# One projection for the keys of two heads, and a score tile with its second pass in two 64-row matmuls

## The chip, the cores and the metric

The kernel runs on one core of one Trainium2 chip. Its time is the device time of one execution in microseconds; before the change it is 985.65 us, the median of three runs (984.38 to 986.23). The engines of the core are TensorE (PE, with PEld for its weight loads), VectorE (DVE), ScalarE (ACT), GpSimd (POOL) and SyncE (SP), which issues most transfers.

## The reference

The program is one transformer layer: cross attention with 16 heads, then a feed-forward part with ternary weights. Of the attention, for two batches of 512 queries and 1024 context rows:

```python
q_hk = (hidden_q @ Wq.T).reshape(Bv, Sv, H, K)
q_big = jnp.einsum('bshk,hkq->bshq', q_hk, w_kc_q)
q_big = _apply_rope(q_big, sin_q[None, :, None, :], cos_q[None, :, None, :])
kv_r = _apply_rope(kv_c, sin_k[None], cos_k[None])
q_r = jnp.einsum('bshq,hqr->bhsr', q_big, W_qr)
k_r = jnp.einsum('bld,hdr->bhlr', kv_r, W_kr)
scores = jnp.einsum('bhsr,bhlr->bhsl', q_r, k_r)
attn = jax.nn.softmax(scores, axis=-1)
ctx_c = jnp.einsum('bhsl,bld->bhsd', attn, kv_r)
ctx_lat = jnp.einsum('bhsd,hkd->bhsk', ctx_c, w_kc_kv)
ctx = ctx_lat.transpose(0, 2, 1, 3).reshape(Bv, Sv, H * K)
return ctx @ Wo.T
```

Queries and keys of a head have R = 64 numbers each. The scores of one head and batch are a 512 x 1024 matrix with a sum over these 64. What follows the attention (a layer norm, two projections with ternary weights, silu, a third projection) is not touched.

## The kernel before

**Precision.** Every operand of a product is held as two parts, hi (the value in the reduced type fp32r) and lo (what hi leaves), and a product is hi x hi + lo x hi + hi x lo, three matmuls (`three`, L852 to L856). After each product ScalarE copies the result from its bank to the hi part (`high_part`, L637 to L655), and VectorE subtracts to get the lo part (`take_out`, L721 to L745).

**Work of a head.** Products of a head are named by a letter and numbers (batch b, tile or half):
- A(b): x times Wq, 12 matmuls of 512 columns. B(b, c): three chunks of the expanded queries, 3 matmuls each; VectorE multiplies them by the rotary tables, GpSimd adds, splits and stores them (`rotate`). C(b): the queries, 6 matmuls (L884 to L891), summed over the rotated chunks.
- K(b, half): keys of a batch, 512 at a time, 3 matmuls each, four groups per head. The weights are given twice side by side (L892 to L896), so rows 0 to 63 and rows 64 to 127 of the result both hold the head's 64 numbers.
- score u, eight tiles of 128 queries and 1024 keys (`score_tile`, L924 to L941): the stationary operand is qr, 128 rows, query hi above query lo. The moving one is kr_hi and then kr_lo, each 128 rows with the keys twice. So a tile is four matmuls of 128 rows and 512 columns.
- max u on VectorE, exp u on ScalarE, T(u, half) the transposes of the exponentials (4 of 128 columns each), V(b) the values (24 matmuls), M the product of two weights, O(b, j) the output tiles (3 matmuls each), which VectorE adds to `acc`.

**What sets the order.** The order is written out by hand in `SCHEDULE` (from L66), one list that TensorE, ScalarE and VectorE all follow, each taking its own items from it. "next" marks a product of the next head that is made ahead and "last" one of the head before that is made late. GpSimd has its own order (`gpsimd_heads`, period, L611 to L632), and so has SyncE. Heads 1 to 14 run in a hardware loop of seven turns with two heads in each; head 0 and head 15 stand apart, the last one in a second block.

**Banks.** The scores have two double banks. All other products share four banks: the long kinds A, C, V one (number 3), the short kinds B, K, T, M, O the other three in turn (`banks_of`, L136). A product can start when the one that used its bank before has been read by VectorE: a wait on `group_read`, which counts the groups in order.

## Time and profile before

| | |
|---|---|
| runs, median (lowest to highest) | 985.65 us (984.38 to 986.23) |
| profiled execution, its own time | 986.32 us |
| its span, first to last instruction | 984.5 us |
| TensorE busy | 879.4 us, 89% |
| VectorE busy | 838.0 us, 85% |
| ScalarE busy | 489.3 us, 50% |
| GpSimd busy | 514.8 us, 52% |
| mean granted TensorE clock | 0.955 |
| heads 1 to 14, from about 110 to 760 us | TensorE busy throughout |

A timeline row gives the start and the length of an instruction in us, the engine, the line of the kernel, the operation, what it writes and reads, and in brackets how long its engine sat idle before it and what ended that. Matmuls overlap: a matmul's row is longer than the distance to the next one's start, and the distance is what it costs. What ran around the change can be read by its tiles: banks<-kt,wk are keys, scores<-kr,qr scores, banks<-ident,probs transposes, banks<-m,cv outputs, banks<-pt,v values, banks<-x,wq A, banks<-rot,wr C.

### The profile page before, as it was taken

To read this page: it belongs to the slowest core of one execution; us is meant where nothing else is said; L and a number is where in the kernel's file an instruction comes from. 1 tells how busy PE (TensorE), PEld (TensorE's weight loads), DVE (VectorE), ACT (ScalarE), POOL (GpSimd) and SP (SyncE) were. 2 spreads that over 40 slices of the span, in tenths; PEclk is the share of its full clock that TensorE was granted. 3 is DMA by queue.
4 is the path that set the end of the run, shared out by engine and by line. 5 is a ranking of instruction groups with operands and counts; after the bars stand their busy time and mean duration, and the time that the engine had idled before them with its cause. 6 is when DMAs were issued, how large, how long until landed. Compare 5 with 4: busy or idle time off the path is not lost. (4 is left out here: it accounts for less than half of the span.)

```text
span 984.5 us, 15195 instructions
## 1 busy us (share of the span) xinstructions
PE 879.4 (89%) x4381; PEld 685.6 (70%) x4390; DVE 838.0 (85%) x1232; ACT 489.3 (50%) x801; POOL 514.8 (52%) x543
## 2 busy tenths in 40 slices
PE   3649999999999999999999999999999776149996
PEld 3437888888888888888888888888888654014443
DVE  6659898989898889999898989898989566979995
ACT  2225455445454545555554545455545587774432
POOL 5277565656565556464646556565656103605541
PEclk9779999999999999999999999999999899559998
DMA  7000000000000101000000000000000650400000
GB/s 272 0 25 25 14 25 14 26 14 24 13 24 13 26 14 30 19 21 16 24 13 24 13 24 24 13 24 13 24 13 24 239 201 4 178 0 12 21 22 32
DMA packets 18262, 38.35 MB, mean 39 GB/s; under 512 B 1600, under 2 KB 8000, under 8 KB 16960
## 3 DMA queue, kind: packets, MB, share of 16 engines
q1 hardware_dynamic: 17152, 35.99, 11.0%
q10 hardware_dynamic: 1088, 2.10, 0.6%
q8 instruction: 11, 0.18, 0.1%
q14 instruction: 11, 0.09, 0.0%
HBM read 35.98 MB, written 2.10 MB: 39 GB/s over the span
## 5 line engine op out<-in xcount | busy, mean ns | idle before, releaser
L664 ACT ACTIVATE probs<-scores,neg_max 128x1024 f32<-128x1024 f32 x128 | 144.1, 1126 | 141.3 <-DVE neg_max L778 140.2
L655 ACT CAST pt_hi<-banks 128x512 fp32r<-128x512 f32 x256 | 144.7, 595 | 126.4 <-PE banks L920 126.4
L745 DVE TENSOR_TENSOR pt_lo<-banks,pt_hi 128x512 fp32r<-128x512 f32 x256 | 169.4, 683 | 20.0 <-ACT pt_hi L655 19.8
L575 POOL TENSOR_TENSOR rot_cos<-rot_cos,rot_sin 128x512 f32<-128x512 f32 x93 | 120.2, 1293 | 117.0 <-DVE rot_sin L754 106.1
L778 DVE TENSOR_REDUCE neg_max<-scores 128x1 f32<-128x1024 f32 x128 | 155.7, 1218 | 1.0
L920 PE MATMUL banks<-ident,probs 128*128 128x128 f32 x1024 | 143.9, 274 | 6.6 <-DVE rot_sin L754 2.3
L920 PEld LDWEIGHTS banks<-ident,probs 128*128 128x128 f32 x1024 | 123.4, 141 | 33.6 <-DVE acc L773 2.8
L583 POOL TENSOR_TENSOR rot_lo<-rot_cos,rot_hi 128x512 fp32r<-128x512 f32 x93 | 119.8, 1288 | 7.8
L937 PE MATMUL scores<-kr_hi,qr 128*128 128x512 f32 x256 | 109.1, 426 | 9.2 <-PEq L983 5.1
L937 PE MATMUL scores<-kr_lo,qr 128*128 128x512 f32 x256 | 102.1, 399 | 0.0
L855 PE MATMUL banks<-pt_hi,v_hi 128*128 128x512 f32 x256 | 100.6, 393 | 1.6 <-DVE pt_lo L745 1.6
L855 PE MATMUL banks<-pt_hi,v_lo 128*128 128x512 f32 x256 | 100.7, 393 | 0.0
L855 PE MATMUL banks<-pt_lo,v_hi 128*128 128x512 f32 x256 | 100.5, 392 | 0.0
L773 DVE SCALAR_TENSOR_TENSOR acc<-banks,inv,acc 128x512 f32<-128x512 f32 x128 | 92.9, 747 | 7.8 <-PE banks L855 7.3
L1432 POOL TENSOR_TENSOR hidden<-sigma,val 128x512 f32<-128x512 f32 x32 | 46.4, 1451 | 60.0 <-DVE val L1346 53.7
L1306 PE MATMUL ps_gv<-ternary,xt 128*128 128x512 bf16 x251 | 59.2, 391 | 14.2 <-PEq L1081 13.2
L752 DVE TENSOR_TENSOR rot_cos<-banks,cos 128x512 f32<-128x512 f32 x96 | 65.8, 685 | 3.5 <-POOL rot_lo L583 2.9
L581 POOL TENSOR_SCALAR rot_hi<-rot_cos 128x512 fp32r<-128x512 f32 x93 | 57.6, 620 | 15.8 <-POOL rot_cos L575 7.5
L855 PE MATMUL banks<-x_hi,wq_hi 128*128 128x512 f32 x128 | 54.8, 428 | 8.0 <-DVE x_lo L404 6.8
L230 POOL TENSOR_SCALAR wv_hi<-load 128x128 fp32r<-128x128 f32 x15 | 4.5, 298 | 109.5 <-PE banks L855 109.5
L937 PEld LDWEIGHTS scores<-kr_hi,qr 128*128 128x128 f32 x256 | 49.0, 191 | 18.0 <-issue 5.3
L855 PEld LDWEIGHTS banks<-pt_hi,v_hi 128*128 128x128 f32 x256 | 48.5, 189 | 12.6 <-DVE pt_lo L745 2.2
(176 smaller groups left out, 1913.6 us busy)
## 6 DMA issues: line engine op xcount, KB each, us to landing
load<-in_pack SPq DMA_DIRECT2D x15, 320.0 KB, 2.9
load<-in_pack SPq DMA_DIRECT2D x16, 256.0 KB, 2.7
raw_early<-in_gate_w SPq DMA_DIRECT2D x4, 1024.0 KB, 8.1
raw_early<-in_val_w SPq DMA_DIRECT2D x4, 1024.0 KB, 15.9
load<-in_pack SPq DMA_DIRECT2D x16, 192.0 KB, 2.4
acc<-in_x ACTq DMA_DIRECT2D x4, 512.0 KB, 7.6
load<-in_pack SPq DMA_DIRECT2D x16, 128.0 KB, 2.1
raw_early<-in_out_w SPq DMA_DIRECT2D x2, 1024.0 KB, 22.2
```

Of the source, the lines that this page charges most:

```text
L575: nc.gpsimd.tensor_tensor(total, total, rot_sin[:, c, :], ALU.add).then_inc(rot_sum, 1)
L583: nc.gpsimd.tensor_tensor(lo, total, hi.bitcast(F32), ALU.subtract).then_inc(rot_ready, 1)
L655: nc.scalar.copy(out, src).then_inc(group_hi, 1)
L664: nc.scalar.activation(probs[:, u % 2, :], scores[:, u % 2, :], ACT.Exp, bias=neg_max[:, u:u + 1], accum_out=sums[:, u:u + 1]).then_inc(ex ...
L745: return nc.vector.tensor_tensor(pair[1], src, pair[0].bitcast(F32), ALU.subtract)
L752: nc.vector.tensor_tensor(rot_cos[:, c, :], src, t["cos"][:, c, :], ALU.mult)
L773: return nc.vector.scalar_tensor_tensor(out=t["acc"][:, u, :], in0=src, scalar=inv[:, u:u + 1], in1=t["acc"][:, u, :], op0=ALU.mult, op1=A ...
L778: nc.vector.tensor_reduce(neg_max[:, u:u + 1], scores[:, u % 2, :], AX, ALU.max, negate=True).then_inc(max_ready, 1)
L855: mm = nc.tensor.matmul(out, ws[a], xs[c], start=first and n == 0, stop=last and n == 2)
L920: mm = nc.tensor.transpose(out[:, c * P:(c + 1) * P], probs[:, u % 2, at:at + P], t["ident"][:])
L937: mm = nc.tensor.matmul(scores[:, u % 2, half * 512:(half + 1) * 512], qr[:, b, j * P:(j + 1) * P], kr[low][:, b, half * 512:(half + 1) * ...
L1306: mm = nc.tensor.matmul(ps_gv[:, n % 4, :], x, w[:, c, part_of(n // 2)], start=c == 0, stop=c == KD - 1)
```

## The change

1. *Keys of two heads in one product.* The weights `wk` now hold three pieces of 64 columns: even head, odd head, even head. K(b, 0) uses the first two and K(b, 1) the last two, so that a group of 3 matmuls gives 512 keys of both heads, one in rows 0 to 63 and the other in rows 64 to 127. `schedule_of` drops the groups that are no longer needed: a head of even number makes K(1, 0) and K(1, 1), an odd one makes K(0, 0) and K(0, 1) for the next pair. Head 15 makes none.
2. *Where the parts lie.* `kr_even` and `kr_odd` take the place of `kr_hi` and `kr_lo`. Each holds one head's keys, hi in one half of the rows and lo in the other (the other way round for the second 512 keys). ScalarE fills the hi parts with two copies of 64 rows, and VectorE the lo parts with two subtractions of 64 rows, from one half of the rows to the other.
3. *Score tile.* `qr_hi` holds query hi in both halves of the rows, `qr_lo` query lo in both. The first pass multiplies qr_hi with 128 rows of keys, hi and lo at once. The second multiplies query lo with key hi alone, 64 rows, rows 0 to 63 for one half of the keys and rows 64 to 127 for the other. The product lo x lo is no longer formed.
4. *Queries.* ScalarE makes two copies of query hi in place of one. VectorE's two steps are as before and fill rows 64 to 127 of qr_lo. A new item "double" is a ScalarE copy of these to rows 0 to 63.
5. *Loading.* Once per pair of heads three transfers bring the key weights to `wk_raw`, and GpSimd splits them in two instructions of 192 columns, instead of two of 128 columns per head.
6. *Space and order.* q and cv share one buffer; O(1, 3) stands ahead of A(1)'s second part. GpSimd's split of the next weights waits for T(1, 1) and not for K(1, 1).

```diff
@@ SCHEDULE
-    ("exp", 0), ("exp", 1), part(1, 2, V1), ("T", 0, 0), ("K", 1, 0),
+    ("exp", 0), ("double", 1, "last"), ("exp", 1), part(1, 2, V1), ("T", 0, 0), ("K", 1, 0),
...
-    ("score", 3), ("max", 3), ("K", 1, 1), ("T", 1, 1), ("O", 1, 2, "last"), part(1, 2, A1), ("T", 2, 0),
-    ("T", 2, 1), ("exp", 3),
-    ("score", 4), ("B", 1, 0, "next"), ("O", 1, 3, "last"), ("T", 3, 0), part(0, 3, C0), part(1, 3, C0),
+    ("score", 3), ("max", 3), ("K", 1, 1), ("T", 1, 1), ("O", 1, 2, "last"), ("O", 1, 3, "last"), part(1, 2, A1),
+    ("T", 2, 0), ("T", 2, 1), ("exp", 3),
+    ("score", 4), ("B", 1, 0, "next"), ("T", 3, 0), part(0, 3, C0), part(1, 3, C0),
...
-    ("score", 6), ("exp", 5), part(0, 8, V0), part(1, 8, V0), part(2, 8, V0), part(3, 8, V0), ("max", 6),
+    ("score", 6), ("exp", 5), ("double", 0, "next"), part(0, 8, V0), part(1, 8, V0), part(2, 8, V0), part(3, 8, V0), ("max", 6),
@@ schedule_of
+        if group[0] == "K" and (group[1] == 0) != odd:
+            return False
...
+        schedule.insert(schedule.index(("exp", 2)), ("double", 1))
@@ weight_splits
-        split(h, 3, [w[:] for w in t["wk"]], twice(src, CQ * R, 1)).then_inc(wk_ready, 1)
+
+    def key_pair(h):
+        pool.wait_ge(t["pair_loaded"], h.pairs(48))
+        pool.nop(nofuse=True)
+        nc.gpsimd.tensor_scalar(t["wk"][0][:], t["wk_raw"][:], 1.0, 0.0, ALU.mult, ALU.add).then_inc(t["pair_hi"], 1)
+        pool.wait_ge(t["pair_hi"], h.pairs(1))
+        nc.gpsimd.tensor_tensor(t["wk"][1][:], t["wk_raw"][:], t["wk"][0][:].bitcast(F32), ALU.subtract).then_inc(wk_ready, 1)
@@ attention_heads
-        qr = sb("qr", [P, B, S], F32R)
-        kr = [placed(f"kr_{x}", [P, B, L], F32R) for x in ("hi", "lo")]
+        qr = [placed(f"qr_{x}", [P, B, S], F32R) for x in ("hi", "lo")]
+        rest = nc.alloc_sbuf_tensor_at("rest", [P, B, S], F32, offset=at["qr_lo"])
+        kr = [placed(f"kr_{x}", [P, B, L], F32R) for x in ("even", "odd")]
...
-        q = [sbe(f"q_{x}", [P, S], F32R) for x in ("hi", "lo")]
+        q = cv
...
+        def keys_at(group):
+
+            _, b, half = group
+            one, other = (x[:, b, half * 512:(half + 1) * 512] for x in (kr[half], kr[1 - half]))
+            return (slice(0, R), one), (slice(R, 2 * R), other)
@@ high_part (ScalarE)
                 elif kind == "C":
-                    out, src = qr[0:R, group[1], :], banks[0:R, p.bank[marked], :]
+                    src = banks[0:R, p.bank[marked], :]
+                    nc.scalar.copy(qr[0][0:R, group[1], :], src)
+                    out = qr[0][R:2 * R, group[1], :]
                 elif kind == "K":
-                    out = kr[0][:, group[1], group[2] * 512:(group[2] + 1) * 512]
+                    (up, into_up), (down, into_down) = keys_at(group)
+                    nc.scalar.copy(into_up[up], banks[up, p.bank[marked], :])
+                    out, src = into_down[down], banks[down, p.bank[marked], :]
...
+            def double(p, marked):
...
+                act.wait_ge(group_read, p.read(done))
+                nc.scalar.copy(qr[1][0:R, b, :], qr[1][R:2 * R, b, :]).then_inc(doubled, 1)
@@ take_out (VectorE)
+                    if kind == "K":
+                        (up, into_up), (down, into_down) = keys_at(group)
+                        nc.vector.tensor_tensor(into_up[down], banks[up, bank, :], into_up[up].bitcast(F32), ALU.subtract)
+                        return nc.vector.tensor_tensor(into_down[up], banks[down, bank, :], into_down[down].bitcast(F32),
+                                                       ALU.subtract)
@@ products and score_tile (TensorE)
-                    pe.wait_ge(wk_ready, h.after(1, 1))
+                    pe.wait_ge(wk_ready, h.pairs(1))
                     at = group[1] * L + group[2] * 512
-                    mm = three(out, [w[:, 0].rearrange("p o r -> p (o r)") for w in wk],
+                    mm = three(out, [w[:, group[2] * R:(group[2] + 2) * R] for w in wk],
                                [t[x][:, at:at + 512] for x in ("kt_hi", "kt_lo")])
...
-                for half in range(2):
-                    for low in range(2):
+                odd = p.head.number % 2
+                if not odd:
+                    pe.wait_ge(group_read, p.read(p.place(("K", 1, 1)) if b else p.earlier(("K", 0, 1, "next"))))
+                pe.wait_ge(doubled, p.head.after(B, b + 1))
+                for low in range(2):
+                    for half in range(2):
+
+                        rows = slice(R * (half ^ odd), R * (half ^ odd) + R) if low else slice(0, P)
                         mm = nc.tensor.matmul(scores[:, u % 2, half * 512:(half + 1) * 512],
-                                              qr[:, b, j * P:(j + 1) * P],
-                                              kr[low][:, b, half * 512:(half + 1) * 512],
+                                              qr[low][rows, b, j * P:(j + 1) * P],
+                                              kr[odd][rows, b, half * 512:(half + 1) * 512],
                                               start=low == 0, stop=low == 1)
```

The order in which instructions stand, at three places of an even head of the loop. A row of it gives the line, the operation, what is written and read (names of the program: kt the rotated context turned round, m and cv the operands of O, ident and probs those of T), the size, and in brackets the semaphores waited for. The first place is TensorE at score 3, before:

```order
L920 MATMUL banks<-ident,probs 128x128 [waits exp_ready]
L920 MATMUL banks<-ident,probs 128x128 x3
L937 MATMUL scores<-kr_hi,qr 128x512 [waits group_read,exp_ready]
L937 MATMUL scores<-kr_lo,qr 128x512
L937 MATMUL scores<-kr_hi,qr 128x512
L937 MATMUL scores<-kr_lo,qr 128x512
```

and after the change:

```order
L974 MATMUL banks<-ident,probs 128x128 [waits exp_ready]
L974 MATMUL banks<-ident,probs 128x128 x3
L992 MATMUL scores<-kr_even,qr_hi 128x512 [waits doubled,group_read,exp_ready]
L992 MATMUL scores<-kr_even,qr_hi 128x512
L992 MATMUL scores<-kr_even,qr_lo 128x512 x2
```

Four matmuls of 128 rows have become two of these and, in the last row, two of 64 rows on qr_lo (the size given is that of the result), and the tile also waits for the new copy.

The second place follows directly behind it on TensorE: K(1, 1), T(1, 1), O(1, 2) and what comes then. Before:

```order
L855 MATMUL banks<-kt_hi,wk_hi 128x512 [waits wk_ready,group_read]
...
L920 MATMUL banks<-ident,probs 128x128 [waits exp_ready,group_read]
L920 MATMUL banks<-ident,probs 128x128 x3
...
L855 MATMUL banks<-m_hi,cv_hi 128x512 [waits group_read]
L855 MATMUL banks<-m_lo,cv_hi 128x512
L855 MATMUL banks<-m_hi,cv_lo 128x512
L855 MATMUL banks<-x_hi,wq_hi 128x512 [waits wq_ready]
```

and after the change:

```order
L909 MATMUL banks<-kt_hi,wk_hi 128x512 [waits wk_ready,group_read]
...
L974 MATMUL banks<-ident,probs 128x128 [waits exp_ready,group_read]
L974 MATMUL banks<-ident,probs 128x128 x3
...
L909 MATMUL banks<-m_hi,cv_hi 128x512 [waits group_read]
L909 MATMUL banks<-m_lo,cv_hi 128x512
L909 MATMUL banks<-m_hi,cv_lo 128x512
...
L909 MATMUL banks<-m_hi,cv_hi 128x512 [waits group_read]
L909 MATMUL banks<-m_lo,cv_hi 128x512
L909 MATMUL banks<-m_hi,cv_lo 128x512
L909 MATMUL banks<-x_hi,wq_hi 128x512 [waits wq_ready]
```

O(1, 3) has moved up. It uses the same one of the three short banks as K(1, 1), and waits for `group_read`; before the change A(1)'s second part stood there, which waits only for its weights.

The third place is VectorE behind V(1), where it takes out the values, T(0, 0) and K(1, 0). Before:

```order
L745 TENSOR_TENSOR cv_lo<-banks,cv_hi 128x512 [waits group_hi]
L726 REGISTER_ALU
L745 TENSOR_TENSOR pt_lo<-banks,pt_hi 128x4x128 [waits group_hi]
L726 REGISTER_ALU
L745 TENSOR_TENSOR kr_lo<-banks,kr_hi 128x512 [waits group_hi]
L769 RECIPROCAL inv<-sums 128x4 [waits exp_ready]
```

and after the change:

```order
L799 TENSOR_TENSOR cv_lo<-banks,cv_hi 128x512 [waits group_hi]
L777 REGISTER_ALU
L799 TENSOR_TENSOR pt_lo<-banks,pt_hi 128x4x128 [waits group_hi]
L777 REGISTER_ALU
L788 TENSOR_TENSOR kr_even<-banks,kr_even 64x512 [waits group_hi]
L789 TENSOR_TENSOR kr_odd<-banks,kr_odd 64x512
L823 RECIPROCAL inv<-sums 128x4 [waits exp_ready]
```

One subtraction of 128 rows (kr_lo) has become two of 64 rows, and only the second is counted as having read the bank.

## Rows read from the trace of the kernel before

**Rows 1.** The page, busy time of each engine (us, share of the span, instructions)
```profile
PE 879.4 (89%) x4381; PEld 685.6 (70%) x4390; DVE 838.0 (85%) x1232; ACT 489.3 (50%) x801; POOL 514.8 (52%) x543
```

**Rows 2.** Busy time by stretch: us and instructions of PE, PEld, DVE, ACT, POOL; PEclk, DMA
```profile
310.00:410.00 100.00, 100.00 (x506) 82.53 (x505) 89.56 (x131) 50.13 (x92) 59.14 (x66) 1.00 0.07 18
```

**Rows 3.** Timeline, GpSimd, one instruction in two heads (start us, us, engine line op, idle)
```profile
341.10 0.62 POOL L230 TENSOR_SCALAR wq_hi<-load 128x512 fp32r<-128x512 f32 x1
...
388.11 0.62 POOL L230 TENSOR_SCALAR wq_hi<-load 128x512 fp32r<-128x512 f32 x1
```

**Rows 4.** Timeline, TensorE, a score tile behind transposes
```profile
302.50 0.48 PE L937 MATMUL scores<-kr_hi,qr 128*128 128x512 f32 x1
302.82 0.40 PE L937 MATMUL scores<-kr_lo,qr 128*128 128x512 f32 x1
303.06 0.40 PE L937 MATMUL scores<-kr_hi,qr 128*128 128x512 f32 x1
```

**Rows 5.** Timeline, VectorE, two 64-row halves of one product
```profile
309.68 0.69 DVE L755 TENSOR_TENSOR rot_sin<-banks,sin 64x512 f32<-64x512 f32 x1
310.39 0.68 DVE L756 TENSOR_TENSOR rot_sin<-banks,sin 64x512 f32<-64x512 f32 x1
```

**Rows 6.** Timeline, the second key group of batch 0, all engines
```profile
341.45 0.40 PE L855 MATMUL banks<-kt_hi,wk_hi 128*128 128x512 f32 x1
...
342.35 0.58 ACT L655 CAST kr_hi<-banks 128x512 fp32r<-128x512 f32 x1 [0.58 <-PE banks L855]
...
342.96 0.69 DVE L745 TENSOR_TENSOR kr_lo<-banks,kr_hi 128x512 fp32r<-128x512 f32 x1 [0.48 <-ACT kr_hi L655]
...
343.71 0.19 PEld L855 LDWEIGHTS banks<-m_hi,cv_hi 128*128 128x128 f32 x1 [0.24 <-DVE kr_lo L745]
```

**Rows 7.** Timeline, the queries of batch 1 and the next first projection
```profile
343.31 0.59 ACT L655 CAST qr<-banks 64x512 fp32r<-64x512 f32 x1
...
344.28 0.68 DVE L731 TENSOR_TENSOR rest<-banks,qr 64x512 f32<-64x512 f32 x1
...
345.82 0.19 PEld L855 LDWEIGHTS banks<-x_hi,wq_hi 128*128 128x128 f32 x1 [0.21 <-issue]
```

**Rows 8.** Timeline, behind the values of batch 1: keys, then a transpose
```profile
311.41 0.48 PE L855 MATMUL banks<-kt_hi,wk_hi 128*128 128x512 f32 x1
...
311.87 0.69 DVE L745 TENSOR_TENSOR cv_lo<-banks,cv_hi 128x512 fp32r<-128x512 f32 x1 [0.80 <-ACT cv_hi L655]
...
313.07 0.68 DVE L745 TENSOR_TENSOR kr_lo<-banks,kr_hi 128x512 fp32r<-128x512 f32 x1
...
314.49 0.60 PE L920 MATMUL banks<-ident,probs 128*128 128x128 f32 x4
```

**Rows 9.** Timeline, the second key group of batch 1
```profile
317.43 1.12 ACT L664 ACTIVATE probs<-scores,neg_max 128x1024 f32<-128x1024 f32 x1
...
317.67 0.39 PE L855 MATMUL banks<-kt_hi,wk_hi 128*128 128x512 f32 x1
...
318.56 0.58 ACT L655 CAST kr_hi<-banks 128x512 fp32r<-128x512 f32 x1
...
319.31 0.68 DVE L745 TENSOR_TENSOR kr_lo<-banks,kr_hi 128x512 fp32r<-128x512 f32 x1
...
319.50 0.40 PE L855 MATMUL banks<-x_hi,wq_hi 128*128 128x512 f32 x1
```

**Rows 10.** Timeline, GpSimd from M to the last rotated part, and its reader
```profile
328.16 0.30 POOL L230 TENSOR_SCALAR wv_hi<-load 128x128 fp32r<-128x128 f32 x1 [7.55 <-PE banks L855]
...
339.85 1.28 POOL L583 TENSOR_TENSOR rot_lo<-rot_cos,rot_hi 128x512 fp32r<-128x512 f32 x1
...
342.50 0.48 PE L890 MATMUL banks<-rot_hi,wr 128*128 128x512 f32 x1
```

**Rows 11.** Timeline, TensorE, the last head
```profile
793.19 1.25 PE L920 MATMUL banks<-ident,probs 128*128 128x128 f32 x8 [1.62 <-DVE kr_lo L745]
```

**Rows 12.** Timeline, TensorE, before the first head
```profile
38.05 0.80 PE L855 MATMUL banks<-x_hi,wq_hi 128*128 128x512 f32 x1 [5.37 <-DVE x_lo L404]
```

More of the change, by code:

```diff
@@ L64 @@
 A0, A1, V1, V0, C0, C1 = ("A", 0, "next"), ("A", 1, "next"), ("V", 1, "last"), ("V", 0), ("C", 0, "next"), ("C", 1, "next")
-UNGROUPED = ("score", "max", "exp", "sum")
+UNGROUPED = ("score", "max", "exp", "sum", "double")
 SCHEDULE = (
@@ L105, in plus, with pairs @@
         return Head(self.number + n, self.i)
+    def pairs(self, per_pair):
+        fixed = (self.number // 2 + 1) * per_pair
+        return fixed if self.i is None else self.i * per_pair + fixed
 def done_by(item):
@@ L167, in __init__ @@
         else:
-            self.schedule = schedule_of(self.first, self.last)
-            self.order, self.bank = order_of(self.schedule), BANK
+            odd = head.number % 2
+            self.schedule = schedule_of(odd, self.first, self.last)
+            self.order, self.bank = order_of(self.schedule), BANK[odd]
             if self.first:
@@ L173, in __init__ @@
             else:
-                self.before = [(g, BANK[g]) for g in ALL]
+                self.before = [(g, BANK[1 - odd][g]) for g in ALL[1 - odd]]
                 self.start = head.after(GROUPS, GROUPS_BEFORE)
@@ L533, in period @@
             def period(p):
+                if p.head.number % 2:
+                    load_key_pair(p.head.plus(1))
                 load_lot(p.head.plus(1), WVO)
@@ L565, in split_wr_wk @@
                 splits[WRK](h, load)
+                if h.number % 2 == 0:
+                    splits[PAIR](h)
             def split_wv_wo(h):
@@ L600, in prepare @@
                 first_split(WRK, start.first_loaded[WRK])
+                splits[PAIR](p.head)
                 rotate_here(0, 2, None)
@@ L682, in prepare @@
                 high_part(p, ("C", 0))
+                double(p, ("double", 0))
                 start.values_high(act, 1)
```

85 lines of the change are left out of this document (47 added, 38 removed).

## The prediction

> **What bounds the kernel now.** I read the page first, then the busy time by stretch, then the timeline of one head on each engine, and last the waits. The page shows TensorE busy 89% of the span and VectorE 85% [rows 1]. In the 100 us from 310 on, TensorE is busy all the time at full clock and VectorE 89.6% [rows 2]; the other stretches between 110 and 760 us are alike. Sixteen heads follow each other. The same GpSimd instruction of two neighbouring heads stands at 341.10 and 388.11, so a head takes 47.0 us [rows 3]. The reader is to see two things. TensorE sets this time, since it never waits for long. But VectorE has only some 4.8 us per head to spare (47.0 x 10.4%), and every product passes through one of four banks that ScalarE and VectorE must first empty. So what the change saves on TensorE counts only as far as the banks are free earlier.
>
> A 512-column matmul starts 0.24 us after the one ahead, though it is recorded as 0.40 long; behind transposes the first takes 0.32 [rows 4]. Over longer stretches it is 0.23: a key group, a group of transposes and an output product fill 317.67 to 319.50 [rows 9] as 3 x 0.23 + 0.44 + 3 x 0.23 = 1.82. I write 0.23 for a pass of 512 columns, 0.69 for a product of three.
>
> **The change, part by part.** My letters are the kernel's: K keys, C queries, A first projection, V attention values, O output, T transpose, M weight product; the numbers are batch, tile or half. A head of even number now makes only K of batch 1, an odd one only K of batch 0.
>
> *TensorE.* Keys: 12 matmuls per head become 6, which takes away 6 x 0.23 = 1.38 us. Scores: per tile, four full passes become two full ones and two of 64 rows. If those two run side by side they cost one pass, and eight tiles save 8 x 0.23 = 1.84 us. A head's TensorE work is then 47.0 - 3.2 = 43.8 us.
>
> *The hand-over of keys.* This is the change's price. ScalarE copies a key group in two halves and only the second signals; VectorE subtracts in two halves that move between partition halves. ScalarE's copies start 0.48 apart back to back (two of them from 342.35 to 343.31) [rows 6, 7], so its signal comes 0.48 later. Two VectorE instructions of 64 rows that shift partitions start 0.71 apart [rows 5], where two of 128 rows took from 311.87 to 313.07, 0.60 each [rows 8]; so a group takes 1.42. Per head that is two groups instead of four, 2.8 against 2.4 us, nearly nothing in busy time. But one group is now released 0.48 + 0.71 = 1.2 us later, and the third short product behind it needs its bank. A queries group adds one ScalarE copy (0.48) ahead of VectorE as well. The two "double" copies per head (2 x 0.5 us) stand where ScalarE idles for VectorE's maximum and I cost them at nothing; without that cover they would put off one exponential by 0.5.
>
> I walk through a pair of heads, in the trace's times.
>
> *Odd head.* (1) The V1 copy goes into the buffer that O(1,0) reads. VectorE starts it at 311.87 [rows 8], its reader is released 0.75 after such a start (342.96 to 343.71 in rows 6): 312.62. With K(1,0) gone, TensorE has only a transpose (0.44 with the slower first matmul) and a score tile (0.69) after V1 ends at 311.05 (one transpose group ahead of 311.41, rows 8), and arrives at 312.18. It waits 0.5. (2) K(0,1) to O(0,3): the weight load had waited 0.24 for this very group, so there is no slack today [rows 6]; 1.2 later means a wait of 1.2, with 0.07 for the exposed weight load 1.3. (3) K(0,0) to T(5,0): 0.2. (4) C1 to the next A: no slack today either (the load sat 0.21) [rows 7]; wait (2) moves TensorE back, 0.1 is left. Together 2.1, the head 43.8 + 2.1 = 45.9.
>
> *Even head.* (5) K(1,0) to T(0,1): VectorE starts at 313.07 today [rows 8], then at about 313.5, and releases at 313.5 + 0.71 + 0.75 = 314.96; TensorE, one score pass earlier, is there at 314.26. Wait 0.8 with the load. (6) K(1,1) to O(1,3), which has moved ahead of A's second part. Today A stands there at 319.50 and waits for no keys. ScalarE can't take the keys before its exponential, 317.43 to 318.56, and VectorE starts at 319.31 [rows 9]. With the second copy and the lateness from (5) it starts near 320.05 and releases at 321.5; TensorE arrives near 319.65 (319.50, three score passes earlier, the wait (5) later, hence 319.50 - 0.69 + 0.85). Wait 1.9 to 2.0. This is the largest term. (7) GpSimd works without a break from M (wv_hi at 328.16) to the last rotated part (339.85 + 1.28 = 341.13), which C1's last part reads at 342.50: slack 1.3 [rows 10]. In an even head TensorE drops three score passes (0.69) and two key groups (1.38) in between: 2.07 - 1.3 = 0.8. (8) C1 to the next A: 0.48 later on ScalarE, a score pass less on TensorE, partly absorbed by (7): 0.3. Together 3.8, the head 47.6.
>
> A pair then takes 93.5 instead of 94.0. So 6.4 us of TensorE work go and 5.9 come back as waits. Where a score pass lies inside one of these windows, making it faster or slower changes nothing; that leaves about 2 tiles of an even and 6 of an odd head that count. The seven pairs of the loop bring 7 x (-0.5) = -3.5 us.
>
> *The cost of turning to 64-row work and back* stands nowhere in this trace. The nearest rows: the first matmul behind transposes starts its follower 0.09 later (0.32 for 0.23) [rows 4], which is an exposed weight load. From below I take nothing (the two 64-row loads hide under the second full pass), from above the whole tail of a matmul, 0.40 - 0.24 = 0.16, with that load, 0.25 a turn and two turns a tile. I take 0.05 a tile, nearest to the row of 0.09, since only some turns should show: 7 x 8 x 0.05 = +2.8.
>
> The Trainium skill, "TensorE: Matmul & The Clock Gate", section "The mechanism", has matmuls on different row groups start about 4 ns apart. No run so far shows it; by it a pair would cost one pass. "TensorEngine Tiling (Array Packing)", section "Key Properties", says that changing the tiling mode drains the array; by it the sum would end on the slower side (rival D, whose price is from the rows above).
>
> *Outside the loop.* Head 0 is even but has no V1 or O waits: between 0 and -3.2, I take -1.5. The last head made K(1,0) and K(1,1) and now makes none; there TensorE sat 1.62 us for K's second part [rows 11]: -2.0 (0 to -3). Its score passes count little, as it waits for others. At the start VectorE subtracts K(0,0) in two parts ahead of x_lo, for which TensorE waits 5.37 us until 38.05 [rows 12]: +0.9, the longer subtraction (0.82), up to +2. The later stages are untouched.
>
> **Sum**, against the profiled execution (986.32 us, span 984.5): -3.5 + 2.8 - 1.5 - 2.0 + 0.9 = -3.3, hence 983.0. The median of the runs is 0.67 lower: 982.3.
>
> **Rivals.**
> A is my forecast. Its own range: with no turning cost 979.5, with 0.11 a tile 985.7, and 4 us either way for waits mis-sized by 0.3 a head: 976 to 990.
> B, the waits are about half as long, because an engine catches up in places that I take as full (VectorE's 10.4% idle speaks for it, the two places with no slack today against it). Then a head drops 3.2 - 1.4 = 1.8: 985.65 - 2.6 - 14 x 1.8 = 958. With no waits at all it would be 938.
> C, the change doesn't do what it says: the 64-row matmuls run one after the other. Each tile costs 0.23 more, four passes as before. By the count above, (2 + 6) x 0.23 = 1.8 a pair, 7 x 1.8 = 13, without the turning term: 982.3 - 2.8 + 13 = 992.5 (990 to 996). Nothing in the trace shows two matmuls side by side, which speaks for it.
> D, slower: every turn between 128-row and 64-row work waits for the array's tail, at the score tiles. Tail 0.16, or 0.25 with the load, twice a tile, gives a tile of 0.69 + 0.32 = 1.01 to 1.19 us against 0.92 before. It decides from 0.10 a turn on, where the tile ceases to be faster than the old one. Over C: 112 tiles x (0.09 to 0.27) = 10 to 30, so 1002 to 1023. Against it: behind transposes no such tail is seen, only 0.09.
> E, the two-part key hand-over starts a chain of waits longer than worked out (each later VectorE step delays the next exponential): 0.8 a head more, 994 to 1000.
>
> **Chances.** A 0.38, B 0.17, C 0.15, D 0.22, E 0.08. This kernel's runs tell a change of about 0.2% (2 us) from none: below 983.7 is faster, above 987.6 slower. A splits into 0.23 faster, 0.09 same and 0.06 slower; B is faster; E, C and D are slower but for 0.08 of the two last, with the waits of A smaller at the same time (0.03 faster, 0.05 same). Faster 0.43, same 0.14, slower 0.43. The range of 8 in 10 leaves out the lower half of B and the upper half of D: 957 to 1008. Cases of both signs hold most of the chance; A's own range is 976 to 990.
>
> **What would show it.** In the changed profile: the third score matmul and the fourth starting together (A) or 0.23 apart (C), and the next full matmul 0.23 behind (A) or 0.4 (D). Key groups: one ScalarE copy and one VectorE start more per group. TensorE's wait for VectorE's keys ahead of an O product, near 1.9 us in even and 1.2 in odd heads; ahead of C1's last part, for GpSimd. Even heads of 47.6 and odd ones of 45.9 us. I am wrong if TensorE stays busy without such waits and the head falls to 44 (B), or if the tile takes over 0.92 us (D).

## The result, and the profile after

Changed kernel: 1023.61 us, median of 4 runs (1021.31 to 1025.91), beside 985.07 us for the kernel before. The ratio is 1.039, 95% interval 1.036 to 1.042: slower. The forecast was 982.3.

The page, and busy time by stretch (columns as in [rows 2]):

```profile
PE 889.9 (87%) x4285; PEld 634.8 (62%) x4294; DVE 846.0 (83%) x1232; ACT 532.6 (52%) x865; POOL 511.1 (50%) x527
```

```profile
310.00:410.00 100.00, 96.84 (x474) 72.30 (x472) 86.90 (x124) 54.13 (x98) 53.58 (x59) 1.00 0.07 19
```

There are 96 fewer matmuls than in [rows 1], yet TensorE is busy 10.5 us longer, and it now has gaps where [rows 2] had none (96.84 of 100 us). PEclk reads 1.00 in both, so the clock is not the cause in the loop. The GpSimd instruction of [rows 3] stands 98.28 us apart over two heads, for 94.0 before:

```profile
308.60 0.63 POOL L242 TENSOR_SCALAR wq_hi<-load 128x512 fp32r<-128x512 f32 x1
...
406.88 0.63 POOL L242 TENSOR_SCALAR wq_hi<-load 128x512 fp32r<-128x512 f32 x1
```

Seven pairs of heads make 30 of the 39.6 us between the two profiled spans (1024.1 and 984.5). The forecast hung on two things. The first is the tile, here TensorE's matmuls and weight loads:

```profile
316.31 0.71 PE L992 MATMUL scores<-kr_odd,qr_hi 128*128 128x512 f32 x2
316.95 0.50 PE L992 MATMUL scores<-kr_odd,qr_lo 64*128 64x512 f32 x2
317.39 0.51 PE L909 MATMUL banks<-cv_hi,wc_hi 128*128 128x512 f32 x1
317.73 0.40 PE L909 MATMUL banks<-cv_lo,wc_hi 128*128 128x512 f32 x1
...
341.27 0.61 PE L992 MATMUL scores<-kr_odd,qr_hi 128*128 128x512 f32 x2
341.82 0.49 PE L992 MATMUL scores<-kr_odd,qr_lo 64*128 64x512 f32 x2
...
316.95 0.19 PEld L992 LDWEIGHTS scores<-kr_odd,qr_lo 64*128 64x128 f32 x2 [0.37 <-issue]
...
317.38 0.19 PEld L909 LDWEIGHTS banks<-cv_hi,wc_hi 128*128 128x128 f32 x1 [0.24 <-issue]
```

The two 64-row matmuls are one row of 0.50 us, where two full ones make a row of 0.71: they do run side by side. But the next full matmul starts 0.44 after them, not 0.23, and its own follower 0.34 after it, not 0.23. Ahead of them, the two full passes of the tile at 341.27 take 0.55 us for 2 x 0.23, which is 0.09 for the turn in. (The tile at 316.31 stands behind transposes, which cost another 0.09 before the change too [rows 4], hence its 0.64.) Each weight load of the other kind begins only with its matmul; between full matmuls it runs 0.2 to 0.25 ahead (317.73 has its load at 317.49). So a tile is 0.46 for two full passes, 0.09 for the turn in, 0.44 for the two 64-row matmuls and what follows them, and 0.11 for the turn out: 1.10 us against 0.92 before.

The second is the keys' hand-over, K(1,1) in an even head, and K(0,1) in an odd one (in time order on each engine):

```profile
382.04 0.58 ACT L688 CAST kr_odd<-banks 64x512 fp32r<-64x512 f32 x1
382.64 0.58 ACT L696 CAST kr_even<-banks 64x512 fp32r<-64x512 f32 x1
...
383.25 0.68 DVE L788 TENSOR_TENSOR kr_odd<-banks,kr_odd 64x512 fp32r<-64x512 f32 x1 [0.38 <-ACT kr_even L696]
383.95 0.69 DVE L789 TENSOR_TENSOR kr_even<-banks,kr_even 64x512 fp32r<-64x512 f32 x1
...
384.69 0.50 PE L909 MATMUL banks<-m_hi,cv_hi 128*128 128x512 f32 x1 [1.55 <-DVE kr_even L789]
...
357.07 0.58 ACT L696 CAST kr_even<-banks 64x512 fp32r<-64x512 f32 x1
...
358.38 0.69 DVE L789 TENSOR_TENSOR kr_even<-banks,kr_even 64x512 fp32r<-64x512 f32 x1
359.13 0.50 PE L909 MATMUL banks<-m_hi,cv_hi 128*128 128x512 f32 x1 [1.09 <-DVE kr_even L789]
```

The weight loads of these two matmuls waited 1.99 and 1.53 us; in [rows 6] the same load waited 0.24. The waits by what ended them, from 160 to 710 us (total us, times, longest):

```profile
PEld scores L992 <- issue: 32.7, 90, 0.4
PEld banks L909 <- DVE kr_even L789: 21.1, 12, 2.0
PEld banks L909 <- issue: 16.1, 62, 0.4
PE banks L909 <- DVE kr_even L789: 15.8, 12, 1.6
```

"issue" is time in which the engine waited for nothing that the profile shows. Here it stands ahead of the 64-row loads of 90 score tiles and of the first full load behind 62 of them: these are the turns. The keys' wait comes 12 times, once a head.

### The profile page after: what moved, and what is told of

The parts are those of the page before. It is cut to its first block and busy times, and to the rows that moved or that the text cites. A ratio compares the mean times of both kernels' runs of the same rounds, so it can differ in the third digit from the quotient of the medians.

```text
span 1024.1 us, 15165 instructions
## 1 busy us (share of the span) xinstructions
PE 889.9 (87%) x4285; PEld 634.8 (62%) x4294; DVE 846.0 (83%) x1232; ACT 532.6 (52%) x865; POOL 511.1 (50%) x527
## 5 line engine op out<-in xcount | busy, mean ns | idle before, releaser
L974 PE MATMUL banks<-ident,probs 128*128 128x128 f32 x1024 | 146.6, 276 | 12.6 <-DVE kr_odd L789 3.4
L974 PEld LDWEIGHTS banks<-ident,probs 128*128 128x128 f32 x1024 | 120.8, 141 | 48.6 <-DVE pt_lo L799 7.4
L799 DVE TENSOR_TENSOR cv_lo<-banks,cv_hi 128x512 fp32r<-128x512 f32 x64 | 44.3, 691 | 75.0 <-ACT cv_hi L696 74.5
L909 PE MATMUL banks<-pt_hi,v_hi 128*128 128x512 f32 x256 | 103.5, 404 | 1.6 <-DVE pt_lo L799 1.6
L696 ACT CAST cv_hi<-banks 128x512 fp32r<-128x512 f32 x64 | 37.5, 586 | 116.3 <-PE banks L909 116.3
L909 PE MATMUL banks<-m_hi,cv_hi 128*128 128x512 f32 x128 | 55.0, 430 | 19.3 <-DVE kr_even L789 18.5
L909 PE MATMUL banks<-x_hi,wq_hi 128*128 128x512 f32 x128 | 55.6, 434 | 10.4 <-DVE x_lo L420 8.5
```

Of the source, the lines that this page charges most:

```text
L696: nc.scalar.copy(out, src).then_inc(group_hi, 1)
L799: return nc.vector.tensor_tensor(pair[1], src, pair[0].bitcast(F32), ALU.subtract)
L909: mm = nc.tensor.matmul(out, ws[a], xs[c], start=first and n == 0, stop=last and n == 2)
L974: mm = nc.tensor.transpose(out[:, c * P:(c + 1) * P], probs[:, u % 2, at:at + P], t["ident"][:])
```

## The experiments

"Pair" is a pair of heads, measured as the distance of the instruction of [rows 3] over two heads inside the loop, "head 0" that from its first to its second place, both from the profiled run, in us. A median and a pair of heads can differ in what they say, since the median also holds head 0, head 15 and the start. All ratios are to the kernel before, on the same chip.

| kernel | pair | head 0 | median us | ratio (95%) |
|---|---|---|---|---|
| before | 94.0 | 44.9 | 984 to 986 | 1 |
| changed | 98.2 | 49.1 | 1023.6 | 1.039 (1.036 to 1.042) |
| a_full_rows | 96.6 | 48.0 | 1010.3 | 1.025 (1.022 to 1.028) |
| b_two_64 | 96.6 | 45.1 | 1004.2 | 1.018 (1.015 to 1.022) |
| b_same_64 | 100.2 | 43.7 | 1033.0 | 1.048 (1.045 to 1.052) |
| b_low_last | 94.0 | 43.4 | 984.7 | 1.000 (0.997 to 1.002) |
| e_one_op | 95.2 | 44.4 | 997.0 | 1.013 (1.010 to 1.016) |
| h_k11_only | 97.0 | 47.2 | 1012.1 | 1.027 (1.024 to 1.030) |
| c_moved | 93.7 | 44.9 | 984.7 | 1.001 (0.999 to 1.002) |
| d_moved_64 | 94.8 | 44.9 | 995.9 | 1.011 (1.008 to 1.013) |
| g_moved_more | 96.6 | 49.4 | 1013.3 | 1.028 (1.025 to 1.031) |
| i_two_moves | 92.9 | 49.6 | 988.8 | 1.002 (1.000 to 1.004) |
| j_max_first | 93.4 | 49.7 | 991.0 | 1.007 (1.005 to 1.010) |
| k_head0 | 93.0 | 44.9 | 986.8 | 1.002 (1.000 to 1.004) |
| m_last_old | 93.0 | 45.0 | 984.3 | 1.000 (0.999 to 1.001) |
| f_busy_last | 98.2 | 49.3 | 1023.4 | 1.039 (1.036 to 1.041) |
| l_head0_busy | 93.0 | 46.2 | 986.5 | 1.002 (1.000 to 1.004) |

Head 0 is one run each, and it differs by 1.5 us between the kernel before and b_low_last, whose medians are the same. So a difference of that size there says little.

### The tile alone

b_low_last puts the low pass last in the kernel before. b_two_64 then gives it 64 rows each, rows 0 to 63 for one half of the keys and 64 to 127 for the other, and b_same_64 the same 64 rows twice; both leave out a part of the low terms. The edit of b_two_64, cut:

```diff
-                for half in range(2):
-                    for low in range(2):
+                for low in range(2):
+                    for half in range(2):
+                        rows = slice(R * half, R * half + R) if low else slice(0, P)
...
-                                              qr[:, b, j * P:(j + 1) * P],
-                                              kr[low][:, b, half * 512:(half + 1) * 512],
+                                              qr[rows, b, j * P:(j + 1) * P],
+                                              kr[low][rows, b, half * 512:(half + 1) * 512],
```

> The kernel before with only the order of a tile's four matmuls changed to that of the changed kernel: both halves with the keys' high part, then both with the low part, all with 128 rows. Theory 1 (it is the turn between 128 and 64 rows): same time as before within 1 us. Rival (it is the order: the accumulation into a bank is interrupted by the other bank): a good part of the 22 us shows here, 995 to 1007 us.

> The kernel before with its score tile alone changed: the pass with the keys' low part comes last and is made of two 64-row matmuls, one on rows 0-63 and one on rows 64-127 (this leaves out part of the product: one half of the low terms for each half of the tile). Everything around the tile is as before, keys and waits too. Theory 1 (turning): 128 tiles by 0.175 us are 22 us more, 1007 us (1003 to 1011). Theory 2 (waits alone): the tile doesn't matter, 983 to 987. Theory 3 (side by side saves as intended, the tile is 0.69 to 0.75 us): 8 x 16 x 0.2 = 25 us less, 960 to 970.

> As the kernel before with the low pass last and as two 64-row matmuls, but both on rows 0-63, so that they can't run beside each other (this leaves out the low terms of rows 64-127). It tells what stands in the 0.44 us of the pair. If they run side by side and 0.21 us of emptying stands beside 0.23 of streaming, two on the same rows take 0.67 us: a tile is 0.23 us longer than with separate rows, 128 x 0.23 = 29 us above the kernel with separate rows, about 1036 us. If they run one after another in both cases, the 0.44 us is 2 x 0.22 and the two kernels take the same time within 2 us.

All three came as the first theory had them. The order of the passes does nothing (984.7). The 64-row pass alone costs 20 us in the kernel before: 2.6 a pair of heads, 0.16 a tile. And with the same rows twice the two matmuls take 0.67 (316.83 to 317.50) where with separate rows they take 0.43 (310.64 to 311.07):

```profile
316.19 0.71 PE L938 MATMUL scores<-kr_hi,qr 128*128 128x512 f32 x2
316.83 0.73 PE L938 MATMUL scores<-kr_lo,qr 64*128 64x512 f32 x2
317.50 0.50 PE L855 MATMUL banks<-q_hi,wc_hi 128*128 128x512 f32 x1
```

```profile
309.99 0.71 PE L938 MATMUL scores<-kr_hi,qr 128*128 128x512 f32 x2
310.64 0.50 PE L938 MATMUL scores<-kr_lo,qr 64*128 64x512 f32 x2
311.07 0.50 PE L855 MATMUL banks<-q_hi,wc_hi 128*128 128x512 f32 x1
```

The first fence is b_same_64, the second b_two_64. One pass more costs 0.24 more, so 0.23 of the 0.44 is one pass and 0.21 is time in which nothing new starts. That this is the array running empty, and not the wait for the weight load that begins so late, no run here separates. Either way a tile with 64-row matmuls pays some 0.4 us for two turns to win 0.23. a_full_rows takes only the 64 rows out of the changed kernel:

```diff
-                        rows = slice(R * (half ^ odd), R * (half ^ odd) + R) if low else slice(0, P)
+                        rows = slice(0, P)
```

> The changed kernel with one expression changed: the second pass of a score tile is made of two 128-row matmuls (the queries' low part stands in both halves, so this adds the product of the two low parts). All else of the change stays. In the trace of the changed kernel the two 64-row matmuls of a tile take 0.44 us together, the turn to them adds 0.09 and the turn back 0.11: a tile is 1.10 us long against 0.92 to 0.97 before. Theory 1 (turning between 128-row and 64-row matmuls empties the array, and this price cancels the shorter keys): each of 128 tiles gets 0.175 us shorter, 22 us in all, 1001 us (997 to 1006, the upper end if the wait for GpSimd, 0.8 us a pair of heads, comes back once the tiles are short). Theory 2 (the tile is not the cause, the time lies in the waits for the keys' longer hand-over alone): the wait takes up what the tile gives, 1020 to 1024 us. Either way 985 would not be reached: some 4.2 us of waits a pair of heads remain.

Neither number was hit: 13 us came back, not 22. A pair got 1.6 shorter where 16 tiles got 2.6 shorter. The missing 1.0 is new waiting: TensorE comes sooner to what isn't ready. T(0,1) waits 0.58 for 0.37, V1's reader 0.24 for 0.13, and T(3,0) some 0.16 more in each head; the rest is in smaller gaps.

### The hand-over of keys

e_one_op copies and subtracts a key group at once in the changed kernel, with 128 rows each, and leaves out the layout of the keys (parts land in the wrong rows). h_k11_only moves K(1,1). Of each edit one part is shown: the ScalarE copies of e_one_op, whose two VectorE subtractions become one in the same way, and the new place of K(1,1).

```diff
-                    (up, into_up), (down, into_down) = keys_at(group)
-                    nc.scalar.copy(into_up[up], banks[up, p.bank[marked], :])
-                    out, src = into_down[down], banks[down, p.bank[marked], :]
+                    out = keys_at(group)[0][1]
```

```diff
-    ("O", 1, 1, "last"), ("T", 0, 1), part(0, 2, A1),
+    ("O", 1, 1, "last"), ("T", 0, 1), ("K", 1, 1), part(0, 2, A1),
```

> The changed kernel with the keys handed over as before the change: one ScalarE copy of 128 rows and one VectorE subtraction of 128 rows a group, in place of two and two of 64 rows (this puts the high and low parts of both heads in the wrong rows: the layout of the keys is left out). The 64-row matmuls and the places of the groups stay. It weighs the hand-over: a group is ready some 0.6 + 0.7 = 1.3 us earlier. Theory (the waits of 1.26 us for K(0,1) in odd heads, 1.7 for K(1,1) in even ones and 0.37 for K(1,0) are the length of the hand-over): the first goes, the second falls to about 0.4, the third goes, so a pair of heads is 3.0 us shorter, 95.2 for 98.2, and the kernel takes about 1000 us (996 to 1004). Rival (the groups would wait for ScalarE's and VectorE's other work anyway, and the place decides): under 1 us a pair, 1016 to 1024.

> The changed kernel with K(1,1) alone moved: from between score 3 and T(1,1) to ahead of the first part of A1, so that A1's six matmuls, T(1,0), score 3 and T(1,1) stand between it and the group that needs its bank. The 64-row instructions and all else stay. Theory (its wait of 1.55 + 0.15 us in even heads is a matter of place): an even head gets 1.4 to 1.9 us shorter, half of that may come back at T(3,0), which then has one group less to hide exp 3 behind; a pair takes 96.4 to 97.4 for 98.2, the kernel 1007 to 1017. Rival (VectorE is full there, the wait turns up whole at T(3,0) or A1): 1020 to 1024.

Both as the theory had it: 3.0 us a pair for the two-part hand-over (997.0), and 1.2 for K(1,1)'s place by itself (1012.1). In h_k11_only an odd head keeps its wait, and K(1,1) itself waits 0.43 in its new place:

```profile
353.43 0.50 PE L909 MATMUL banks<-m_hi,cv_hi 128*128 128x512 f32 x1 [1.08 <-DVE kr_even L789]
372.01 0.66 PE L974 MATMUL banks<-ident,probs 128*128 128x128 f32 x4 [0.19 <-DVE kr_odd L789]
373.10 0.51 PE L909 MATMUL banks<-kt_hi,wk_hi 128*128 128x512 f32 x1 [0.43 <-DVE acc L827]
```

### Full rows and moved groups

c_moved has a_full_rows' tile, d_moved_64 the changed kernel's, both with these moves (cut):

```diff
-("exp", 1), part(1, 2, V1), ("T", 0, 0), ("K", 1, 0),
+("exp", 1), ("K", 1, 0), part(1, 2, V1), ("T", 0, 0),
-("T", 3, 0), part(0, 3, C0), part(1, 3, C0),
+part(0, 3, C0), ("T", 3, 0), part(1, 3, C0),
-part(0..3, 8, V0), ("max", 6), part(4, 8, V0), ("K", 0, 0, "next"), part(5, 8, V0)
+part(0..1, 8, V0), ("max", 6), part(2, 8, V0), ("K", 0, 0, "next"), part(3..4, 8, V0), ("K", 0, 1, "next"), part(5, 8, V0)
```

(and K(1,1) as in h_k11_only; `0..3` stands for a run of parts).

> The kernel with full rows (1010.3 us, a pair of heads 96.6) with the key groups elsewhere in the order: K(1,0) ahead of the second part of V1, K(1,1) ahead of the first part of A1, K(0,0) and K(0,1) behind parts 3 and 5 of V0, and the first part of C0 ahead of T(3,0). Theory (after the shorter keys and full rows are counted, all that is left over the 91.2 us a pair should take, 94.0 less 12 matmuls of 0.23, is waits that follow from where the groups stand): a pair takes 91.5 to 92.5 us and the kernel 965 to 975, faster than before the change. Rival (ScalarE and VectorE have no room for the added 64-row instructions, so that the waits only turn up elsewhere, at the softmax of the tile that follows): a pair stays at 94 or above, 985 to 1005.

> The changed kernel, 64-row matmuls and all, with the same moves of the key groups. Theory (turning and waits simply add): a pair is 16 x 0.163 = 2.6 us longer than with full rows, 94.1 to 95.1, and the kernel takes 985 to 997; even without waits it is then no faster than before the change. Rival (the turning costs only where the array has no other gap, so it overlaps part of what waited): within 8 us of the kernel with full rows and the same moves.

c_moved fell between the two: a pair of 93.7, no faster than before. 2.8 us of keys are gone from TensorE and 2.5 us of waits are left. The largest, in an odd head, shows VectorE's queue: both key groups wait behind the maxima and rotary products, and T(5,0) waits for K(0,1).

```profile
331.15 0.39 PE L909 MATMUL banks<-kt_hi,wk_hi 128*128 128x512 f32 x1
...
333.57 1.23 DVE L832 TENSOR_REDUCE neg_max<-scores 128x1 f32<-128x1024 f32 x1
334.83 0.68 DVE L788 TENSOR_TENSOR kr_even<-banks,kr_even 64x512 fp32r<-64x512 f32 x1
...
337.77 0.65 PE L974 MATMUL banks<-ident,probs 128*128 128x128 f32 x4 [0.78 <-DVE kr_even L789]
```

d_moved_64 took 995.9, inside its range, but not for its reason: turns and waits do not simply add. The turns cost 1.1 a pair of heads there and not 2.6 (11 us in all, with the heads outside the loop).

g_moved_more moves T(5,0) behind score 7, T(0,1) ahead of O(1,0) and C1's last part ahead of T(6,0); i_two_moves only the first two. The first of the moves:

```diff
-    ("T", 4, 1), ("T", 5, 0),
-    ("score", 7), part(0, 3, C1),
+    ("T", 4, 1),
+    ("score", 7), ("T", 5, 0), part(0, 3, C1),
```

> The kernel with full rows and moved key groups (984.7 us, a pair 93.7), with three groups more moved, each where its trace shows TensorE waiting: T(5,0) behind score 7 (it waited 0.78 us for K(0,1)'s subtractions), T(0,1) ahead of O(1,0) (0.24 to 0.5 for V1's low part), the last part of C1 ahead of T(6,0) (A0 waited some 0.2 for C1). Theory (TensorE bounds a pair at 91.2, the rest is single waits): a pair takes 91.7 to 92.8, the kernel 966 to 978, faster than before the change. Rival (VectorE, busy without a gap for the 17 us from C0 to the end of V0 in odd heads, bounds that stretch, and its queue sets the pair): a pair stays above 93.2, 981 to 986.

> The kernel with full rows and moved key groups (984.7 us, a pair 93.7) with T(5,0) behind score 7 and T(0,1) ahead of O(1,0), and C1's last part back where it stood: in the last kernel, with a pair of 96.6, T(6,1) waited 1.60 us a head for T(6,0)'s subtraction, which had come to stand behind C1's copies. Theory (that wait alone made that kernel slow, the two other moves gain their 0.8 and 0.3 to 0.5 us): 2 x 1.6 less and some 0.2 back at A0, a pair takes 92.4 to 93.4, the kernel 974 to 982. Rival (VectorE's queue sets the pair, whatever is moved): a pair 93.6 to 94, 983 to 987.

g_moved_more missed the upper end of its range by 35 us. In the loop, 2.9 a pair of heads, it was a wait that I had not looked for, 1.6 us in every head: T(6,1) waits for T(6,0)'s subtraction, held behind C1's copies. Head 0 took 4.5 us more as well.

```profile
307.99 0.66 PE L974 MATMUL banks<-ident,probs 128*128 128x128 f32 x4 [1.60 <-DVE pt_lo L799]
```

i_two_moves hit its pair (92.9) and missed its time (988.8, forecast 974 to 982). Head 0 took 4.7 us of it (49.6 for 44.9); even without them it would have stood above 982.

### The ends

j_max_first swaps `("max", 2)` and T(0,1) on VectorE; k_head0 puts K(1,1) between O(1,0) and O(1,1); m_last_old is k_head0 with T(0,1) and T(5,0) back in their old places in head 15; f_busy_last and l_head0_busy issue the transposes of tiles 2 and 3 of head 15 three times (in the changed kernel and in k_head0):

```diff
-                    for c in range(4):
+                    for n in range(4 * (3 if p.last and u in (2, 3) else 1)):
+                        c = n % 4
```

> The last kernel with VectorE's maximum of tile 2 ahead of T(0,1)'s subtraction instead of behind it (TensorE's order is unchanged). In the last kernel a pair of heads in the loop took 92.9 us, 1.1 less than before the change, yet head 0 took 49.6 where it takes 44.9: TensorE waited 2.27 and 2.76 us there, and the granted clock of 80 to 88 us was 0.63. Theory (head 0 lost by the order of those two on VectorE, and by the lower clock after its waits): head 0 returns to 44.9 to 46 us, a pair stays at 92.9 to 93.4, the kernel takes 978 to 983. Rival (head 0's waits hang on the start, not on this order): head 0 stays above 48, 985 to 989.

> As the kernel of 988.8 us (full rows, moved groups, a pair 92.9), with K(1,1) between O(1,0) and O(1,1) instead of behind both. In the two kernels before this one head 0 took 49.6 us where it had taken 44.9, because head 0 has no O(1,*) groups: K(1,1) there follows T(0,1) at once in the same bank and waited 2.76 and 5.21 us for it. With K(1,1) in the bank of T(0,0) that wait should go. Theory (head 0's loss, in the changed kernel too, is a bank's hand-over and the lower clock that follows such a wait, not the start): head 0 takes 44.5 to 46.5 us, a pair stays at 92.9 to 93.4, the kernel takes 978 to 984. Rival (head 0's time hangs on when the first lots come in): head 0 stays at 48 to 50, 986 to 990.

> The kernel of 986.8 us (full rows, all moves, a pair 93.05, head 0 44.9) with T(0,1) and T(5,0) back in their old places in the last head alone. In the loop that kernel gained 0.95 us a pair over the kernel before, 6.7 us; in the profiled run the last head's first tile to the next stage's first transposes took 85.6 us for 83.4, with waits of 1.20, 0.63 and 2.67 us where the kernel before has 0.20 to 1.10. Theory (the moves that serve the loop cost the last head, where fewer groups stand between, some 2 to 3 us): with the old places these waits go, that stretch takes 83 to 84.5 us and the kernel 983 to 985. Rival (the last head is set by the softmax and by the clock, not by these places): 986 to 988.

> The changed kernel with TensorE kept busy in the last head: the transposes of tiles 2 and 3 are issued three times over there (the same result each time; 32 transposes more, 3.6 us of TensorE's time, put where it waited 1.5, 1.0 and 1.9 us). Theory (the last head is 3.8 us longer than before the change because TensorE idled before M, and the clock then granted was 0.50 to 0.74 for 13 us): no stretch at a lower clock follows, and from score 4 of the last head on its matmuls are 0.23 us apart; the stretch from the last head's first tile to the first matmul of the next stage takes 62 to 64.5 us for 65.8, and the whole 1020 to 1023. Rival (the low clock has another cause): the stretch at a low clock stays, and the last head gets longer by what of the 3.6 us doesn't fit the waits, 1023 to 1027.

> The same kernel with the transposes of tiles 2 and 3 of the last head issued three times over (same result), 3.6 us of work where TensorE otherwise waits some 5 us. Theory (as in the changed kernel, whose last head became 1.8 us shorter by this, the granted clock stays up when TensorE is kept busy): the stretch of 8 us behind tile 3 shows a clock of 1.00 where it was 0.79 to 0.81, and the kernel takes 1 to 3 us less than the one beside it, 976 to 982. Rival (the added work eats what the clock gives): the same within 1 us, or up to 3 us longer.

*Head 0.* j_max_first: the theory fell, head 0 stayed at 49.7, and the wait got longer (5.21 us, for 2.76 in i_two_moves). k_head0: with another bank for K(1,1) head 0 is at 44.9 and the pair at 93.0, as forecast, though the wait is shorter (1.79) and not gone, and the time (986.8) is not the forecast one. So for head 0 of these moved kernels it was the bank: head 0 has no O(1,*), and K(1,1) came right behind the transposes that hold it. In the changed kernel K(1,1) stands elsewhere, and e_one_op speaks for its head 0. j_max_first, then k_head0:

```profile
83.12 0.79 PE L909 MATMUL banks<-kt_hi,wk_hi 128*128 128x512 f32 x1 [5.21 <-DVE pt_lo L799]
```

```profile
80.51 0.50 PE L909 MATMUL banks<-kt_hi,wk_hi 128*128 128x512 f32 x1 [1.79 <-DVE pt_lo L799]
```

*Head 15.* From its first score tile to the next stage's first transposes: before 83.4 us, changed 87.4 (808.81 to 896.18), f_busy_last 85.6. Busy time and granted clock of three stretches, the changed kernel and then f_busy_last:

```profile
828.00:835.00 7.00, 3.39 (x21) 2.28 (x21) 4.17 (x7) 5.13 (x8) 0.00 (x0) 0.96 1.02 392
835.00:841.00 6.00, 6.00 (x14) 3.35 (x15) 4.35 (x5) 4.92 (x6) 0.00 (x0) 0.50 0.13 45
841.00:848.00 7.00, 7.00 (x26) 5.56 (x25) 0.25 (x1) 1.83 (x5) 0.00 (x0) 0.74 0.00 0
```

```profile
828.00:835.00 7.00, 5.33 (x43) 4.68 (x44) 3.34 (x5) 4.01 (x6) 0.00 (x0) 1.00 1.02 390
835.00:841.00 6.00, 5.30 (x28) 3.47 (x27) 4.19 (x6) 4.70 (x9) 0.00 (x0) 1.00 0.05 18
841.00:848.00 7.00, 6.82 (x37) 5.30 (x35) 2.92 (x5) 5.55 (x11) 0.00 (x0) 1.00 0.00 1
```

Behind the idle stretch the clock was at 1.2 GHz (0.50) and with useless work in it at 2.4 GHz (1.00); 1.8 us of the stretch came back in the profiled run, but the median (1023.4) doesn't tell it from nothing. Behind tile 3 in k_head0, and then in l_head0_busy:

```profile
796.00:804.00 8.00, 7.76 (x27) 6.32 (x28) 4.86 (x6) 6.56 (x9) 0.00 (x0) 0.79 0.02 5
```

```profile
797.00:805.00 8.00, 7.29 (x42) 6.00 (x43) 4.57 (x6) 6.61 (x10) 0.00 (x0) 1.00 0.01 4
```

The clock rose to 1.00, as the theory had it, but no time came back (986.5 for 986.8), which is what the rival said. M (banks<-wo_hi,wv_hi) started 31.1 us behind the head's first tile, for 27.9 in k_head0, so the added transposes cost more than the 1 to 3 us that the clock was to give. m_last_old got its time (984.3) but not its reason: the stretch that should shrink to 83 to 84.5 took 86.3 in the profiled run, for 85.6 in k_head0. The runs of k_head0 spread from 984.2 to 990.4, so what the last head costs it stays open, and so does why 1.0 us less for a pair of heads, 7 us over the loop, showed in no median. No version beat the kernel before.

## Why the prediction was wrong

*The score tile.* This step failed. Right: the two 64-row matmuls run side by side. Wrong: "a score tile (0.69)" with "0.05 a tile" for turning. Measured: 1.10 a tile, 0.41 more. Over the 16 tiles of a pair of heads that is 6.6 us, where the forecast had 0.4 (0.05 for each of the 8 tiles that it thought would count). Less the 1.6 by which the waits came out smaller, this gives 4.6; a pair of heads missed by 4.3 (98.2 for 93.9), 30 us over the loop. The other 11 of the 41 us missed are head 0 and head 15. My lower bound supposed that the 64-row weight loads hide under the full pass; they don't (the load engine stands still for 0.37 us ahead of them and for 0.24 behind, once each in a tile). I took the row of 0.09 for the whole price because the trace had a row for it, and gave the bound of 0.25 a turn only the rival. The turns sum to 0.41 a tile, 0.09 in, 0.21 ahead of the next full matmul, 0.11 behind it, against my upper bound of 0.50. b_two_64 shows that this cost is not hidden: with nothing but the 64-row pass changed, the kernel is 20 us longer.

*The rivals.* D named this cost with 1.01 to 1.19 a tile and 1002 to 1023 us; the tile came out inside, the time just above. "TensorEngine Tiling (Array Packing)", section "Key Properties", in the Trainium skill says that a change of tiling mode drains the array. The 20 us of b_two_64 agree with that, though they don't show what the array does. Rival C is dead by b_same_64: matmuls one after the other take 0.67, these 0.44. "TensorE: Matmul & The Clock Gate", section "The mechanism", in the Trainium skill has matmuls on different row groups start about 4 ns apart. The trace agrees as far as one row of 0.50 for both can tell. B had half the waits (about 3 a pair of heads) and a fast tile; the waits were 4.3 and the tile slow. E had more waiting than forecast; there was less.

*Keys on TensorE*, -1.38 a head: right; 94.0 - 2.8 + 16 x 0.17 + the waits of 4.3 is the 98.2 seen (0.17 is what a tile takes over the old 0.92: 0.16 by b_two_64, 0.18 by the rows).

*Waits*, 5.9 a pair forecast, 4.3 seen by this sum. (2) 1.3: 1.26 seen. (6) 1.9 to 2.0: 1.7. (5) 0.8: 0.37; (1) 0.5: 0.13; (3) 0.2: none; (4) and (8) together 0.4: 0.15. (7), 0.8 for GpSimd: none; the tiles that had to be faster were slower, which may be why. Not foreseen: T(3,0) waits 0.25 in the odd and 0.26 in the even head for exp 3; O(1,3) had moved from ahead of it, which no run tests by itself. The mechanism, a longer hand-over in a place with no slack, is shown by e_one_op, which took 3.0 of the 4.3 away. ScalarE's two copies stand 0.60 apart, not 0.48, and VectorE's two subtractions 0.70, as forecast. That only a part of the tiles' time counts where waits stand was right in kind: 1.6 of 2.6 in a_full_rows, 1.1 of 2.6 in d_moved_64. (The spare time of VectorE, given as 4.8 us a head, is 4.9 by its own terms, 47.0 x 10.4%; no term of the sum uses it.)

*Outside the loop.* Head 0: -1.5 forecast, +4.2 seen; e_one_op takes it to 44.4, so it is mostly the keys' hand-over (a_full_rows, with the old tile, leaves it at 48.0), and between 80 and 96 us TensorE is busy 11.6 of 16 us for 15.0 before. Head 15: -2.0 forecast, +3.9 seen. An estimate puts 1.3 of it on the eight slower tiles (8 x 0.16 from b_two_64), and 1.8 was gone in the one profiled run with the clock up; the rest is open. The start: +0.9 forecast; the first wq_hi behind it stands between 61.2 and 63.1 us in all 17 profiled runs, whichever keys they use (61.2 before the change, 63.1 after it, 63.0 in m_last_old), so it can't be told.

*The range.* The likeliest case let turning vary only from 0 to 0.11 a tile, though its price was the one that stood in no row; the bounds were 0 and 0.50, and the likeliest case should have spanned them.

## What to carry to other kernels

A cost that no row shows deserves the widest bounds, not the value of the nearest row: here 0.05 a tile, which should have been 0.41, came 112 times in the loop. One pair of 64-row matmuls between full ones did not pay here: it won one pass of 0.23 and paid 0.41. By these numbers, and this is an estimate that no run tests, two such pairs in a row (0.46 won) would about break even. And taking work off the busiest engine of a balanced kernel can move the wait to the next queue: 2.8 us less on TensorE for a pair of heads were never worth more than 1.1.

## What the runs showed of the hardware

- Two 512-column matmuls on rows 0 to 63 and 64 to 127 together take 0.43 to 0.44 us between full ones (b_two_64 and the changed kernel), two on the same rows 0.67 (b_same_64).
- Turning from 128-row to 64-row matmuls and back costs 0.41 us in the changed kernel, and no weight load of the other kind runs ahead: it starts with its matmul (316.95, 317.38), where loads between full matmuls start 0.2 to 0.25 us ahead.
- Half the rows did not make an instruction shorter. Two ScalarE copies of 64x512 start 0.60 us apart (382.04 and 382.64) and two VectorE subtractions 0.70 (383.25 and 383.95); two of 128x512 start 0.48 and 0.60 apart before the change [rows 6, 7, 8]. For ScalarE the gap goes with the change of rows: in the changed kernel a 64-row copy that begins at row 0, like the 128-row one ahead of it, starts 0.48 behind that (357.68, 358.16), and the next one, which writes rows 64 to 127, 0.59 behind it (358.75).
- In head 15 the granted clock went from 1.00 to 0.50 (2.4 to 1.2 GHz) behind three waits of TensorE of 1.53, 0.99 and 1.94 us with transposes between them, and stayed at 1.00 in f_busy_last, where the waits were 1.52, 0.97 and 0.19 and more transposes stood between them. In the kernel before, waits of 1.62 and 1.94 us at the same place had left it at 1.00.
